# Edges of a two-stage layer reordered; in each element of its attention stage four steps change places on TensorE, VectorE and ScalarE

## The reference, cut to what matters

```
q  = Wq @ layernorm(x);  k = Wk @ ctx;  v = Wv @ ctx          # 8 heads of 64
q  = softmax over the 64 of a head, * 64**-0.5;  k = softmax over the 1024 positions
context = k @ v^T per head;  out = Wo @ (context^T @ q) + bo
x  = x + tanh(g_xattn) * out / norm(out over channels) * g * sqrt(128)
s  = layernorm(x) @ Wr^T;  gates = softmax of the 16 largest of 64, 0 elsewhere
x  = x + tanh(g_ffn) * 2 * sum over experts of gate * B (A layernorm(x))
```

## Time and profile before

| | us |
|---|---|
| median of 3 runs | 905.81 |
| profiled execution | 906.83 |
| its span in the profile | 905.1 |
| TensorE busy | 882.1 (97%) |
| VectorE busy | 742.8 (82%) |
| ScalarE busy | 678.4 (75%) |
| GpSimd busy | 543.8 (60%) |

### The profile page before, as it was taken

One profiled execution on the slowest core, in us unless ns is written; L12 is line 12 of the kernel. 1 busy time (PEld: TensorE's weight loads), 2 busy tenths in 40 slices (PEclk: granted clock), 3 DMA queues, 4 the chain that ended last, 5 costly groups with the idle time before them and its releaser, 6 DMA issues.

```text
span 905.1 us, 15780 instructions
## 1 busy us (share of the span) xinstructions
PE 882.1 (97%) x4604; PEld 742.8 (82%) x4604; DVE 742.8 (82%) x1515; ACT 678.4 (75%) x1392; POOL 543.8 (60%) x374
## 2 busy tenths in 40 slices
PE   6899999999999999999999899999999999999998
PEld 4677877888888888888877788889899989999996
DVE  5899899899889989998897878887778778877642
ACT  4877887788778777877886758588888878888731
POOL 3697797799899989988899956232222212222100
PEclk9999999999999999999999999999999999999999
DMA  4434645654674557354632894212221212211001
GB/s 162 164 102 156 211 139 162 213 177 166 185 239 153 180 164 227 122 164 162 192 103 94 293 347 147 70 70 71 71 71 71 71 59 75 76 65 52 24 24 47
DMA packets 46846, 120.88 MB, mean 134 GB/s; under 512 B 5712, under 2 KB 21072, under 8 KB 46800
## 3 DMA queue, kind: packets, MB, share of 16 engines
q1 hardware_dynamic: 41040, 99.37, 32.9%
q0 software_dynamic: 5472, 20.45, 7.1%
q10 hardware_dynamic: 288, 0.52, 0.2%
HBM read 87.82 MB, written 32.51 MB: 133 GB/s over the span
## 4 chain that ended last, share of the span: by engine, by line
PE 67%; DVE 10%; POOL 9%; issue 7%; ACT 5%; DMA 2%; DVEq 0%; POOLq 0%; ACTq 0%
PE ps L61 20%; PE ps L62 19%; PE ps L63 19%; PE ps L1579 4%; PE ps L1570 3%; ACT h_raw L835 3%; PE ps L1560 2%; POOL qe L490 1%; DMA aT_hi<-in_AT 1%; POOL xn_lo L456 1%; POOL ctxT_lo L449 1%; POOL qhalf L475 1%; POOL x L570 1%; POOL qe L485 1%; POOL qT_lo L495 1%
## 5 line engine op out<-in xcount | busy, mean ns | idle before, releaser
L567 POOL TENSOR_TENSOR rb<-u_in,rb 128x1024 f32<-128x1024 f32 x14 | 33.7, 2405 | 216.0 <-DVE rb L1060 216.0
L61 PE MATMUL ps<-aT_hi,yT_hi 128*128 128x448 f32 (+2 forms) x360 | 119.4, 332 | 2.0 <-DVE hg L1220 1.4
L62 PE MATMUL ps<-aT_hi,yT_lo 128*128 128x448 f32 (+2 forms) x360 | 118.1, 328 | 0.0
L63 PE MATMUL ps<-aT_lo,yT_hi 128*128 128x448 f32 (+2 forms) x360 | 118.0, 328 | 0.0
L835 ACT ACTIVATE h_raw<-hg 32x256 f32<-32x256 f32 x248 | 103.1, 416 | 17.3 <-DVE hg L1253 14.5
L835 ACT ACTIVATE y_raw<-u_in 32x256 f32<-32x256 f32 x216 | 89.5, 415 | 7.0 <-DVE u_in L1236 4.6
L61 PE MATMUL ps<-bT_hi,hT_hi 128*128 128x512 f32 x240 | 93.7, 390 | 0.0
L62 PE MATMUL ps<-bT_hi,hT_lo 128*128 128x512 f32 x240 | 93.5, 390 | 0.0
L63 PE MATMUL ps<-bT_lo,hT_hi 128*128 128x512 f32 x240 | 93.4, 389 | 0.0
L490 POOL TENSOR_TENSOR qe<-qe,qrec 128x1024 f32<-128x1024 f32 x48 | 91.3, 1902 | 1.4 <-DVE qrec L1082 1.4
L731 ACT ACTIVATE qe<-ps 128x1024 f32<-128x1024 f32 x48 | 49.1, 1024 | 42.1 <-PE ps L1560 42.1
(11 more groups left out here) (186 smaller groups left out, 2671.5 us busy)
## 6 DMA issues: line engine op xcount, KB each, us to landing
x_in<-in_x SPq DMA_DIRECT2D x16, 512.0 KB, 4.3
ctx_in<-in_ctx SPq DMA_DIRECT2D x16, 512.0 KB, 5.6
ctxT_in<-in_ctxT SPq DMA_DIRECT2D x16, 512.0 KB, 4.3
ctxT_hi<-in_ctxT POOLq DMA_DIRECT2D x16, 512.0 KB, 3.7
turn_q_scratch<-qe SPq DMA_DIRECT2D x16, 512.0 KB, 2.6
qe<-turn_q_scratch SPq DMA_DIRECT2D x64, 128.0 KB, 2.9
u_scratch<-osb SPq DMA_DIRECT2D x16, 512.0 KB, 2.9
x<-in_x SPq DMA_DIRECT2D x15, 512.0 KB, 4.0
```

Source lines behind the costliest of these rows:

```text
L61: nc.tensor.matmul(psum, whi, mhi, start=start, stop=False)
L62: nc.tensor.matmul(psum, wlo, mhi, start=False, stop=False)
L63: return nc.tensor.matmul(psum, whi, mlo, start=False, stop=stop)
```

## The change

In the loop of elements 2 to 13 (and in 14 and 15 likewise): VectorE does `scale_m(b-1)` ahead of `lo_q(b-1,1)`, and `max_k(b,2)` ahead of `max_q(b,1)`; TensorE does `shift_q(b,1)` behind the first half of `output(b-1,0)`; ScalarE's `out_o(b-1,0)` moves behind `hi_k(b,3)` (not in 15).

Element 0: on TensorE `fold_weights` is earlier, and `mm_q(0,3)` and `mm_k(1,0)` change places; on VectorE `lo_k(0,3)` and `max_q(0,3)` go ahead of `sum_q(0,1)` and `max_k(1,0)`; on GpSimd the split of ctxT is ahead of the first normalisation. Element 1 (`second`): `max_q(1,0)`, `lo_kc(0)` and `max_k(1,1)` come first, and `sum_q(0,3)`, `stats(2)` and its first steps behind `max_q(1,1)`. Element 14: `lo_kc` ahead of `early_guess`. Element 15: `lo_k(15,3)` ahead of a sum and the steps of a root, the last loads of `aT_hi` ahead of a normalisation. Expert stage: `sum_u(7)` behind the second piece of `up(5)`, the first round of TensorE's loop is written out, and in body 1 `stats2_sums` is ahead of `lo_moved_h(1)`.

```diff
@@ -580,9 +580,14 @@
                     lo_moved_q(b - 1)
                 if tail:
                     normalise(b - 1, 2)
+                if head and not started(b):
+                    hi_c(b)
                 if head:
                     halve(b, 0)
-                if tail:
+                if head and not started(b):
+                    lo_c(b)
+                second = isinstance(b, int) and b == 1
+                if tail and not second:
                     normalise(b - 1, 3)
                 if tail and not head:
+                if second:
+                    normalise(b - 1, 3)
                 if head and started(b):
                 if head:
                     normalise(b, 0)
-                    hi_c(b)
+                    if started(b):
+                        hi_c(b)
                 if head:
                     halve(b, 1)
-                    lo_c(b)
-                if head and not ahead:
-                    spread_first(1)
+                    if started(b):
+                        lo_c(b)
                 if ahead:
                     lo_xn(b + 1, 0)
-                if head:
                     normalise(b, 1)
-                if head and not ahead:
+                    halve(b, 2)
+                elif head:
+                    spread_first(1)
                     for t in range(3, DC):
                         hi_a(t)
-                if head:
+                    normalise(b, 1)
                     halve(b, 2)
+                    add_first(1)
                 if isinstance(b, int) and b == NB - 2:
                     early_newton()
-                if head and not ahead:
-                    add_first(1)
 
...
-                if tail:
+                if tail and not (isinstance(b, int) and b == 1):
                     exp_q(b - 1, 3)
...
                     exp_k(b, 1)
+                    if not started(b):
+                        act.wait_ge(fold_done, 1)
...
                     scale_first(1)
-                if tail and head:
-                    out_o(b - 1, 0, early)
+                    out_o(b - 1, 0)
                 if head:
                     exp_q(b, 2)
-                    if not started(b):
-                        act.wait_ge(fold_done, 1)
-                        for par in range(2):
-                            nc.scalar.activation(wvo[0][:, :, par * P:par * P + P],
-                                                 psX[:, par, :].rearrange("p (j o) -> p j o", o=P),
-                                                 ACT.Copy, scale=DH ** -0.5).then_inc(fold_hi, 1)
-                if head:
                     hi_k(b, 2)
-                if ahead:
+                if ahead and not started(b):
+                    hi_k(b, 3)
+                    hi_xn(b + 1, 0)
+                    exp_q(b, 3)
+                    exp_k(b + 1, 0)
+                elif ahead:
                     hi_xn(b + 1, 0)
                     exp_k(b + 1, 0)
-                if head:
+                if head and started(b):
                     hi_k(b, 3)
+                if tail and ahead:
+                    out_o(b - 1, 0, early)
                 if tail and not head:
                     hi_y(1)
...
+                second = isinstance(b, int) and b == 1
                 if tail:
                     sum_q(b - 1, 2)
+                if second:
+                    max_q(b, 0)
+                    lo_kc(b - 1)
+                    max_k(b, 1)
                 if head and turned(b):
                     turn_k(b)
-                if ahead and started(b):
+                if ahead and started(b) and not second:
                     stats(b + 1)
-                if ahead and started(b):
                     std(b + 1, range(3))
-                if tail:
+                if tail and not second:
                     sum_q(b - 1, 3)
-                if head and started(b):
+                if head and started(b) and not second:
                     max_q(b, 0)
+                if tail and not second:
+                    lo_kc(b - 1)
                 if norms:
                     early_guess()
-                if tail:
-                    lo_kc(b - 1)
-                if head and started(b):
+                if head and started(b) and not second:
...
+                if tail:
+                    scale_m(b - 1)
                 if tail and head:
                     lo_q(b - 1, 1)
-                if tail:
-                    scale_m(b - 1)
...
-                if head:
+                if head and started(b):
+                    max_k(b, 2)
+                    max_q(b, 1)
+                elif head:
                     max_q(b, 1)
                     max_k(b, 2)
+                if second:
+                    sum_q(b - 1, 3)
+                    stats(b + 1)
+                    std(b + 1, range(3))
                 if head:
...
+                if ahead and started(b):
+                    max_k(b + 1, 0)
                 if last:
                     dve.wait_ge(xn_lo, 2 * NB)
                     spread(1, rb_first[1], n_newton, 4 * NEWTON)
-                if ahead:
-                    max_k(b + 1, 0)
                 if head:
                     lo_k(b, 2)
+                if last:
+                    stats2_sums(0, 0)
                 if not started(b):
                     low_fold()
-                if last:
-                    stats2_sums(0, 0)
-                if head:
-                    sum_q(b, 1)
-                if last:
-                    std2(0, range(4))
-                if head:
                     lo_k(b, 3)
                     max_q(b, 3)
-                if last:
-                    std2(0, range(4, NCH + 1))
+                    sum_q(b, 1)
+                    max_k(b + 1, 0)
+                elif head and not last:
+                    sum_q(b, 1)
+                    lo_k(b, 3)
+                    max_q(b, 3)
+                elif last:
+                    lo_k(b, 3)
+                    sum_q(b, 1)
+                    max_q(b, 3)
+                    std2(0, range(NCH + 1))
...
+                if norms:
+                    stats2_sums(b + 2, (j + 3) % SLOTS)
+                if first:
                     lo_moved_h(1)
                 if norms:
-                    stats2(b + 2, (j + 3) % SLOTS)
+                    std2(b + 2, range(NCH + 1))
...
+                    if not started(b):
+                        fold_weights()
-                if head and turned(b):
-                    shift_q(b, 1)
                 if tail and head:
                     output(b - 1, 0, range(CH // 2))
-                if head and not turned(b):
+                if head:
                     shift_q(b, 1)
-                    if not started(b):
-                        fold_weights()
-                if ahead:
+                if ahead and started(b):
                     mm_k(b + 1, 0)
                 if head:
                     tr_k(b, 2, next(turn))
+                if head and not started(b):
+                    mm_q(b, 3)
                 if tail and head:
                     output(b - 1, 1, range(CH // 2))
                 if head:
                     tr_k(b, 3, next(turn))
+                if head and started(b):
                     mm_q(b, 3)
+                elif head:
+                    mm_k(b + 1, 0)
...
-                late = isinstance(i, int) and b in (1, 2, 4)
+                late = isinstance(i, int) and b in (1, 2, 4, 5)
-            with pe.Fori(1, NB // SLOTS - 1) as i:
+            for j in range(SLOTS):
+                ffn_body(1, j)
+            with pe.Fori(2, NB // SLOTS - 1) as i:
                 for j in range(SLOTS):
                     ffn_body(i, j)
```

More of the change, by code:

```diff
@@ L896, in body @@
                     exp_k(b, 1)
+                    if not started(b):
+                        act.wait_ge(fold_done, 1)
+                        for par in range(2):
+                            nc.scalar.activation(wvo[0][:, :, par * P:par * P + P],
+                                                 psX[:, par, :].rearrange("p (j o) -> p j o", o=P),
+                                                 ACT.Copy, scale=DH ** -0.5).then_inc(fold_hi, 1)
                 if tail:
```

## The result

The changed kernel takes 915.13 us in the median of 4 runs (914.87 to 915.56), the kernel before 906.51 beside it (905.75 to 908.09): a ratio of 1.0077, 95% interval 1.0053 to 1.0101. It is slower, by 8.6 us. The profiled execution took 915.56 with a span of 913.8, against 905.1.

What follows compares the result with a forecast made beforehand. VectorE's run up to chunk 1's low half was taken to set each element's length. The terms summed to +7.1 us on the profiled 906.83, so 913.9; the median forecast was 913 us, range 907 to 918.

Steps and rivals of the forecast that it cites:

- The loop: Elements 5 to 13: VectorE waits for fold, then for mm_k(b,2); each element 0.81 longer, +7.3 us.
- All of that lies ahead of mm_k(9,0), so it brings 0: Loop: earlier M scaling and output, and shift_q(b,1) waiting for pair 1's maximum, change nothing, as VectorE's run sets mm_k(9,0).
- Element 0: Start: TensorE and VectorE reach the first context earlier, at 35.5 instead of 38.55; -3.0 us (bounds -1.9 and -3.4).
- Element 1: Steps costing 3.40 move inside VectorE's run, so the element takes 35.4; +3.4 us (bounds 0 and +4).
- Elements 2 to 4, 14: Elements 2 to 4 take 31.83 each, together +0.3 us; element 14 becomes about 32.0, +0.3 us.
- Element 15 and the loads: End of attention: lo_k(15,3) goes ahead, -0.4 us; last aT_hi loads start some 2 us earlier, -0.4 (bounds -1 and 0).
- Experts: Expert stage: late sum_u(7) no longer waits; of its 1.68 us 0.4 is kept, -0.4 (bounds 0 and 1.7).
- The return of VectorE's loop takes it back: Expert stage, element 9: VectorE's 3.87 us of issue sets the pace again, and TensorE waits longer for part_u(11).
- Rival A: Loop: the chain from M to the output, not VectorE's run, holds TensorE; 895 us, chance 0.12.
- B: Loop: the wait for fold is hidden elsewhere, the loop is unchanged, elements 0 and 1 cancel; about 905 us, chance 0.08.
- C: Loop as forecast, but the pile of steps in element 1 is hidden; 909.5 us, chance 0.12.
- D: Loop: ScalarE's moved copy out_o comes too late for the context, 0.6 more an element; 918.4 us, chance 0.04.

Runs made afterwards that it cites:

- new_order: Changed kernel minus the three loop edits, element 15's new VectorE order and early aT_hi loads; element 2's layernorm start moved earlier in element 1: 902.66 us, ratio 0.9957.

## Why the prediction was right, and where it was wrong

Sign and size came out (913 for 915.1), but the size partly by luck: in the pair of profiles the loop, element 0 and the expert stage together came out 3.2 below my terms for them, and the tail behind context 15 5.3 above.

- **The loop** (+7.3, measured 9 x 0.70 = +6.3). The mechanism was right in each step: wait for fold, low half and maximum 2 behind it, then the law "one us later on VectorE, one us longer". Mis-sized is a term: I kept 2.39 for the two maxima, and they cost 276.69 - 274.42 = 2.27. It is the scaling's place that makes it so and not the maxima's: in element 8 they cost 2.26 to 2.28 in the seven traces with the scaling first, in either order of the maxima, and 2.38 or 2.39 in the seven without. This 0.12 is also why the scaling alone cost 0.58 and not 0.69. What makes it is open.
- **"All of that lies ahead of mm_k(9,0), so it brings 0"** held only for this combination. The late shift is what keeps TensorE from standing 1.57 for pair 1's maximum; without it the change would have cost 1.15 an element. And I followed the late shift on TensorE alone: its own 0.48 reached VectorE through ScalarE's queue.
- **Element 0** (-3.0): -4.0 in the one pair of profiles, but over all profiled executions the first context starts at 38.5 with the old head (five, 37.9 to 39.1) and 35.3 with the new one (nine, 34.5 to 36.5): -3.2.
- **Element 1** (35.4, measured 35.47): the number was right, the cause only half. I made it of the pile of 3.40 moved inside VectorE's run, and chunk 1's low half does end at 27.22 behind the context, to the digit. But GpSimd was as late: TensorE waits 2.52 in this element for its low half of xn, which I had not named, and with VectorE's run 2.2 shorter (new_order, 25.04) the element became only 0.37 shorter. With the order taken back it takes 35.24: those steps then stand ahead of pair 0's maximum, where "VectorE had time" was true only while element 0 was long. Element 0's gain is owed in either order; what gets 1.7 of it back is the sum put early.
- **Elements 2 to 4, 14** (31.83 and 32.0): 31.72 and 31.92, the loop's 0.1 again.
- **Element 15 and the loads** (-0.4 and -0.4) is the step that failed. The element became 0.66 shorter, but the way from context 15 to sum_u(3) 3.0 longer on average (38.4 to 39.7 before, 40.5 to 44.4 after), 4.9 in the pair of profiles. I asked what the earlier steps release and not what they push back: sum 1, and with it GpSimd's normalisation and kc's low half, and x's second half, whose load was now issued behind 2.7 MB of aT_hi.
- **Experts** (-0.4, measured -1.5). "The return of VectorE's loop takes it back" was wrong: that return is unchanged (3.84 of issue), but the wait at sum_u(11) did not grow (0.42, before 0.52), as VectorE itself comes earlier with TensorE: its result(7) starts 157.10 behind sum_u(4), before 158.62. The written-out round on TensorE brought nothing that can be seen.

Rival A fell with the run of the scaling alone, B with the contexts 31.72 apart, C with 35.47 in element 1. D did not occur: with the loop's edits taken back and out_o late the elements are 31.02.

## What to carry to other kernels

Put a step at the head of an in-order queue only when its input is there: an early step that waits 1.37 delays everything behind it, and here the whole element. Find the point at which the waiting engine picks up the other one's result, and price edits by how much later that point comes; but follow a moved step to every engine that waits for it (the late shift did its harm on ScalarE), and test the edits in pairs, since one that costs alone may be what makes another affordable. When a start-up gets shorter, ask which engine's backlog was hidden in it.

## What the hardware showed that I had not expected

- **A load issued 0.7 us behind others took twice as long.** DMA issues from 6 us before to 14 us behind context 15 (queue, count, KB each, us to landing), the changed kernel and then the one before:

```profile
aT_hi<-in_AT POOLq DMA_DIRECT2D x5, 544.0 KB, 11.5
x_second<-in_x SPq DMA_DIRECT2D x1, 512.0 KB, 9.5
```

```profile
aT_hi<-in_AT POOLq DMA_DIRECT2D x5, 544.0 KB, 8.1
x_second<-in_x SPq DMA_DIRECT2D x1, 512.0 KB, 4.4
```

  Over six kernels x's sum starts 6.6 to 10.1 behind context 15, and by and large the later, the later SP issued the load behind the aT_hi loads (0.34 to 1.05). The Trainium skill, DMA: Bandwidth & Descriptors, section on queues, rings and completion order, says that each DMA engine goes round the queues that have work, a packet at a time. By an estimate from that rule, with packets alike in both queues and no other work in SP's, SP's 0.5 MB would land when about 1 MB had moved in all, some 4 us at the 209 to 309 GB/s that the trace has between 516 and 523. It took 9.5: the trace does not agree with this estimate, and no run here shows why.
- **The clock fell at the start in some executions and not in others.** Windows of new_order and then of the changed kernel without the scaling first, whose programs and first matmuls agree up to here (both start mm_q(0,0) 12.5 us in, after 1.4 us of waiting); the last three columns are granted clock, DMA share and GB/s:

```profile
12.00:14.00 2.00, 1.55 (x7) 1.32 (x8) 0.33 (x1) 1.64 (x4) 0.30 (x1) 1.00 1.02 412
14.00:16.00 2.00, 2.00 (x9) 1.15 (x7) 1.89 (x3) 0.38 (x3) 1.83 (x2) 1.00 0.09 35
```

```profile
12.00:14.00 2.00, 1.54 (x5) 1.31 (x6) 0.34 (x1) 1.62 (x3) 0.31 (x1) 0.79 1.01 393
14.00:16.00 2.00, 2.00 (x6) 1.51 (x6) 1.22 (x2) 0.39 (x3) 1.82 (x2) 0.50 0.20 80
```

  In the second TensorE runs at its lower level from 13.3 to 16.3, and the first shift starts at 16.87 instead of 15.39. In all fourteen profiles the shift starts either 10.4 or 11.8 us behind the arrival of x_in, which itself comes at 5.0 to 6.0: five have the fall (two with the old head, three with the new). The two together make the spread of the first context, 1.2 with the old head and 2.0 with the new; one profile of each kernel is not enough to price an edit at the start.
